# A graph layer and a feed-forward layer: ScalarE evicts y_hi of a tile in the tile's seventh slot instead of the next tile's second

## The reference, cut to what matters

```
x = x + gnn(layernorm(x), src, dst, W_self, W_neigh, b)
x = x + ffn(layernorm(x), w_gate, w_up, w_down)

gnn: msg_sum = segment_sum(x[src], dst);  neigh = msg_sum / max(deg, 1)
     h = leaky(x @ W_self + neigh @ W_neigh + b);  return h / max(norm(h), 1e-12)
ffn: each weight is made ternary in groups of 128 inputs:
     scale = mean(|w|) + 1e-5;  wq = clip(round(w / scale), -1, 1) * scale
     return (silu(x @ gate.T) * (x @ up.T)) @ down.T
```

## Time and profile before

| what | value |
|---|---|
| median of three runs | 386.58 us (386.08 to 388.95) |
| the profiled execution's own time | 388.67 us |
| its span (first to last instruction) | 386.8 us |
| PE busy | 348.7 us, 90% |
| DVE busy | 321.6 us, 83% |
| ACT busy | 250.5 us, 65% |
| POOL busy | 166.4 us, 43% |
| mean granted clock of TensorE | 0.972 |

### The profile page before, as it was taken

The page is one execution under the profiler, slowest core; times in us unless marked ns, Lnnn a source line. Parts: engine busy times, 40 slices in busy tenths (PEclk is TensorE's granted clock), DMA queues, the critical chain, the costliest instruction groups (busy, mean ns, idle before and its releaser), DMA issues.

```text
span 386.8 us, 5916 instructions
## 1 busy us (share of the span) xinstructions
PE 348.7 (90%) x1741; PEld 261.9 (68%) x1741; DVE 321.6 (83%) x748; ACT 250.5 (65%) x667; POOL 166.4 (43%) x214
## 2 busy tenths in 40 slices
PE   1989988979999899999975899999999999999972
PEld 1435544535554448777765789899899899889962
DVE  2598887977989502899968799999999999999983
ACT  2265757666777311577465787897897897788740
POOL 3011342221232110212001228588888879878982
PEclk9998999989999989999999999999999999999995
DMA  7941212222122100120000000000000000000034
GB/s 236 261 138 56 56 54 81 68 58 65 59 75 73 33 3 3 28 75 20 3 1 0 2 0 2 1 3 0 2 1 3 1 0 2 1 3 0 2 108 159
DMA packets 9415, 16.73 MB, mean 43 GB/s; under 512 B 1062, under 2 KB 1886, under 8 KB 9378
## 3 DMA queue, kind: packets, MB, share of 16 engines
q1 hardware_dynamic: 9378, 16.29, 14.9%
HBM read 13.73 MB, written 2.56 MB: 42 GB/s over the span
## 4 chain that ended last, share of the span: by engine, by line
PE 53%; DVE 24%; ACT 9%; POOL 5%; issue 5%; DMA 2%; POOLq 0%; SPq 0%; ACTq 0%; DVEq 0%
PE bank L1170 35%; PE bank L1061 6%; PE bank L1107 5%; DVE hot_dst L881 5%; DVE tq_gu L817 4%; ACT mag_early L628 3%; DVE hot_src L877 2%; POOL acc L599 2%; ACT hot_src L613 2%; DVE tq_d L817 2%; PE bank L1023 2%; PE bank L1091 2%; DMA w_sb<-in_L_gnn_W_neigh 2%; DVE bn L922 1%; DVE x_sb L919 1%
## 5 line engine op out<-in xcount | busy, mean ns | idle before, releaser
L1170 PE MATMUL bank<-x_hi,t_gu 128*128 128x378 f32 (+1 forms) x264 | 95.8, 363 | 2.0 <-DVE x_lo L936 1.3
L1170 PE MATMUL bank<-x_lo,t_gu 128*128 128x378 f32 (+1 forms) x264 | 94.6, 358 | 0.0
L1061 PE MATMUL bank<-w_sb,xnT 128*125 128x512 f32 x160 | 88.4, 640 | 1.4 <-DMA w_sb<-in_L_gnn_W_neigh 1.4
L599 POOL TENSOR_TENSOR acc<-acc,d_one 128x378 f32<-128x378 f32 (+1 forms) x84 | 88.3, 1077 | 0.7 <-ACT d_one L728 0.3
L561 POOL TENSOR_SCALAR thr<-absum 128x4 f32<-128x4 f32 (+1 forms) x34 | 12.2, 358 | 129.5 <-ACT mag_early L628 89.5
L1023 PEld LDWEIGHTS bank<-hot_dst,hot_src 128*125 128x125 bf16 x281 | 32.0, 139 | 52.0 <-DVE hot_dst L881 33.5
L971 DVE SCALAR_TENSOR_TENSOR g_acc<-bank,nscale,g_acc 128x378 f32<-128x378 f32 (+1 forms) x99 | 63.9, 646 | 3.7 <-PE bank L1170 3.3
L586 POOL TENSOR_TENSOR hh<-sg,u_acc 128x378 f32<-128x378 f32 (+1 forms) x32 | 35.2, 1100 | 66.4 <-ACT sg L750 62.6
L971 DVE SCALAR_TENSOR_TENSOR u_acc<-bank,nscale,u_acc 128x378 f32<-128x378 f32 (+1 forms) x99 | 63.6, 642 | 0.0
L1170 PEld LDWEIGHTS bank<-x_hi,t_gu 128*128 128x128 f32 x264 | 50.2, 190 | 6.7 <-DVE x_lo L936 2.0
L1170 PEld LDWEIGHTS bank<-x_lo,t_gu 128*128 128x128 f32 x264 | 50.4, 191 | 3.6
(11 more groups left out here) (107 smaller groups left out, 548.3 us busy)
## 6 DMA issues: line engine op xcount, KB each, us to landing
raw<-in_L_ffn_w_gate SPq DMA_DIRECT2D x11, 256.0 KB, 2.9
raw<-in_L_ffn_w_up SPq DMA_DIRECT2D x11, 256.0 KB, 2.6
out_x<-x_sb SPq DMA_DIRECT2D x10, 224.0 KB
raw<-in_L_ffn_w_down SPq DMA_DIRECT2D x8, 256.0 KB, 2.6
x_sb<-in_x SPq DMA_DIRECT2D x1, 1344.0 KB
w_sb<-in_L_gnn_W_neigh SPq DMA_DIRECT2D x1, 1024.0 KB, 7.1
w_sb<-in_L_gnn_W_self SPq DMA_DIRECT2D x1, 1024.0 KB, 8.6
raw<-in_L_ffn_w_down SPq DMA_DIRECT2D x4, 192.0 KB, 2.3
```

The source lines that it names most:

```text
L599: nc.gpsimd.tensor_tensor(to, to, d_one[:, o, slot, 0:width(u)], ALU.add).then_inc(d_added, 1)
L1061: last = nc.tensor.matmul(to[0:TP, :], xnT[:, t, k * TP:(k + 1) * TP], w_sb[:, k, half * D:(half + 1) * D], start=k == 0, stop=k == KD - 1)
L1170: last = nc.tensor.matmul(to, w, parts[h], start=h == 0, stop=h == 1)
```

## The change

ACT's eviction of y_hi moves within the loop over slots. Before, y_hi of tile t - 1 was evicted at i = 1 of tile t; now y_hi of tile t is evicted at i = 6 of tile t itself, three slots earlier. The semaphores it waits for and signals, the bank it reads and the tile it writes are the same, and so are all other instructions and all other engines' programs.

```diff
-                if i == 1 and 1 <= t <= NT:
-                    act.wait_ge(y_ready, t)
-                    nc.scalar.activation(y_hi[:, t - 1, :], bank[4 + (t - 1) % 2][0:TP, :], ACT.Copy).then_inc(yhi_done, 1)
+                if i == 6 and t < NT:
+                    act.wait_ge(y_ready, t + 1)
+                    nc.scalar.activation(y_hi[:, t, :], bank[4 + t % 2][0:TP, :], ACT.Copy).then_inc(yhi_done, 1)
```

## The result

The changed kernel took 377.25 us, the median of four runs (375.62 to 378.46), against 386.44 us (386.08 to 388.95): a ratio of 0.9748, with a 95% interval of 0.9706 to 0.9790. It is 9.2 us faster. The profiled execution took 377.23 us; its span fell by 11.5 us, from 386.8 to 375.3.

What follows compares the result with a forecast made beforehand. The prediction took DVE's y_lo waits for ACT's y_hi, with PE waiting behind for one-hot tiles, to bound the stage. It summed -7.67 + 0.58 + 0.67 = -6.4 us, from 386.58 to 380.2 us, range 377.4 to 385.6.

Steps and rivals of the forecast that it cites:

- That y_lo would wait no more: On DVE, all six waits of y_lo for y_hi inside the stage should go: -7.67 us.
- That the last one was worth next to nothing: The last tile's y_lo wait, 3.35 us, lies under PE's degree sums; its removal was costed at nothing.
- The margin before y_ready: On ACT, y_hi in the seventh slot comes 8 us after PE's matmuls, so its wait costs nothing.
- +0.58: Magnitude jobs behind the new y_hi come later; one late POOL scale makes DVE wait 0.58 us more.
- +0.67: ACT's hot_src is delayed by the moved y_hi; one more DVE wait for it, 0.67 us.
- the sum: The forecast's total over the stage: -7.67 + 0.58 + 0.67 = -6.4 us, called 85% of the waits.
- Rival A: Late scales in the ACT, POOL, DVE ring take most back: gain 3.6 us, 383.0 us; chance 0.25.
- I take 0 to +0.8 and count it at nothing: TensorE's clock dip after the pause at 81.48 might go, winning up to 0.8 us; counted at nothing.
- The two limits, 11.38 and 11.10: Time per tile: DVE without its y_lo waits 11.38 us, PE with little to wait for 11.10 us.
- PE can give back at most 74.87 - 66.60 = 8.27 us: Over six tiles from 43.39 us, PE can gain at most 8.27 us before it sets the pace.
- Rival B: PE takes the pace at 11.10 us a tile, giving the whole 8.27 us: 378.3 us; chance 0.08.

Runs made afterwards that it cites:

- the repeats: The kernel before and the changed kernel, each run again unchanged with one execution for a second trace: 387.74 us and 377.01 us.
- ylo_later: The kernel before with DVE's y_lo two slots later and y_hi in its old place on ACT: 378.37 us, ratio 0.9716.
- z_last: The changed kernel with POOL's ten additions of the bias to z made only after the last z is evicted: 372.56 us, ratio 0.9617.
- before_z_last: The kernel before with POOL's additions of the bias made after the last z: 379.68 us, ratio 0.9784.
- tile4_old: The changed kernel with y_hi of tile 4 alone back in the old place: 381.16 us, ratio 0.9803.
- tile4_z_last: z_last with y_hi of tile 4 in its old place: 373.34 us, ratio 0.9673.
- split_stats: The changed kernel with the LayerNorm statistics of tiles 4 to 9 taken in two groups of three: 379.15 us, ratio 0.9791.

## Why the prediction was right or wrong

**That y_lo would wait no more** was right: all six waits are gone, the last tile's too but for 0.5 us. That the last one was worth next to nothing fits: of the 10.6 us between the spans of the repeats, the start (0.3) and the seven tiles (9.96) leave 0.3. ylo_later shows that the wait was nearly the whole matter, 9.0 of the 9.96 us.

**The margin before y_ready** was right: no wait of ACT for PE at y_hi appears.

**"+0.58" for a scale and "+0.67" for hot_src** were charged to the sum and not paid. Measured were +0.7 for the scales in all (1.8 less 1.1; 0.4 in the repeats, 1.8 less 1.4) and 0 to 0.4 for hot_src. Together these are 0.7 to 0.8 us of waits where 1.25 were charged, and in the tile-by-tile table no tile pays for them: where a wait of y_lo went, the tile got shorter by at least as much, and the slow tile and the one after it together by 4.69 us for 3.62. So the 1.25 us should have been near nothing. Rival A, with a chance of 0.25, was given too much: another 0.5 us of ACT's work at the same place made the seven tiles 0.8 us longer.

**"I take 0 to +0.8 and count it at nothing"**, the clock, is the step that failed. I had seen the pause at 81.48, the one-hot tile of 1.32 us and the 0.50, and treated them as three things, two of them constant. They came and went together: with the wait of tile 4 alone restored the second pause, the 1.32 us and the 0.50 were back, and that wait of 1.74 us cost 3.33; with the additions out of the stage the pause was 0.44, the clock stayed, and the cost was 0.97, in two pairs of kernels. Over the six waits the part beyond their own length is 9.96 - 7.67 = 2.3 us (1.6 in the first pair), of which 1.1 lies in the tile with the slow stretch and the one after it, and 0.93 in the first tile. How much of it is the fallen clock and how much the second pause was not separated.

With the 1.25 us that were not paid, the sum comes out: 6.4 + 1.25 + 2.3 = 9.96. The fall from 9.96 to 5.71 without the additions holds both this surplus and the 1.8 us of waits (7.54 - 5.71) that did not reach PE.

**"The two limits, 11.38 and 11.10"** were wrong, and they set the fast end of the range: "PE can give back at most 74.87 - 66.60 = 8.27 us". DVE's 11.38 held its wait for PE in the slow stretch and the additions; it came to 11.13. PE's 11.10 was its quickest tile beside a DVE that held it back, and not what PE needs: PE went at 10.52 a tile in z_last, where it was busy without a break. Rival B named the right size, 8.1 against 8.27 in those six tiles, for the wrong cause; DVE still sets the pace after the change, as taking the additions off it shows. And both were counted only from 43.39 us: more lay before it. In the repeats, where no slow stretch hides it, tile 2 to tile 3 fell from 12.52 to 10.55 us, 1.97 of which 1.04 is the wait of y_lo. The other 0.93 goes with the additions: in the kernel before one of them, at 29.20, also fell on a conversion, and in before_z_last, without them, this tile is only 0.96 over z_last. Which addition it is was not tested.

Two slips change nothing: 6.4 is 84% of 7.67 and not 85%, and in ACT's queue ahead of y_hi a finished block stood too.

**The base.** The profiled execution of the kernel before had a slow stretch at 30 to 34 us that its repeat lacks, and the fall in its span, 11.5 us, is larger than the 10.6 between the repeats. The medians give 9.2; why both pairs of spans give more is open.

## What to carry to other kernels

A wait on the engine that feeds TensorE is priced by its own length only while the feeder sets the pace and nothing else follows from the wait. Ask how far the feeder is ahead, and what else falls on it once that lead is gone: part of a wait may vanish in the lead, and a wait that makes TensorE stop twice in a row may cost its length again. A tile's quickest time beside a second engine of nearly the same pace is not a floor of either; take away the other's load to see it.

## What the runs showed of the hardware

POOL's addition of the bias (1.26 to 1.42 us) held up a DVE operation that ran beside it by about 1 us: a one-hot tile took 1.32 us instead of 0.32. What the Trainium skill says in SBUF — State Buffer, Who interferes with whom, that whoever comes second at the ports that the two engines share is held until the first is done, agrees with that number. Taking the ten additions out of the stage gave 1.3% with the change and 2.2% without it.

The granted clock went to 0.50, the 1.2 GHz level, after two pauses of 1.19 and 1.44 us with 0.39 us of matmuls between them (tile4_old), and stayed at 1.00 after one of 0.44 (tile4_z_last), and also around two longer ones, 1.77 and 1.49 us, that had 3.2 us of nearly unbroken matmuls between them (split_stats). Whether the stretch at 30 to 34 us came differed between executions of the same kernel.
